# Attention with routed experts on one core: in the step that splits the next context, the keys projected in rounds 2 and 3, in the bank that the queries leave

## What is computed

```python
def xattn(query, key, value, ...):            # B = 8, S = 512, D = 512, H = 16, Hd = 32
    Q, K, V = split_heads(query @ Wq.T + bq), split_heads(key @ Wk.T + bk), split_heads(value @ Wv.T + bv)
    attn = softmax(einsum('bhqd,bhkd->bhqk', Q, K) / sqrt(Hd))
    return merge_heads(einsum('bhqk,bhkd->bhqd', attn, V)) @ Wo.T + bo
x = x + xattn(layernorm(x), ctx, ctx, ...)    # keys and values from the context
x = x + experts(layernorm(x), ...)            # router softmax, top 2 of 8, gated feed-forward, weighted sum
```

## Time and profile before

| | us |
|---|---|
| median of three executions | 1665.96 |
| lowest, highest | 1665.07, 1674.82 |
| the profiled execution | 1670.91 |
| its span in the trace | 1669.2 |
| PE busy | 1583.9 (95%) |
| DVE busy | 1308.7 (78%) |
| POOL busy | 836.0 (50%) |
| ACT busy | 692.8 (42%) |

### The profile page before, as it was taken

The page is one execution under the profiler, slowest core; times in us unless marked ns, Lnnn a source line. Parts: engine busy times, 40 slices in busy tenths (PEclk is TensorE's granted clock), DMA queues, the critical chain, the costliest instruction groups (busy, mean ns, idle before and its releaser), DMA issues. The chain is left out here.

```text
span 1669.2 us, 30419 instructions
## 1 busy us (share of the span) xinstructions
PE 1583.9 (95%) x9607; PEld 1162.8 (70%) x9607; DVE 1308.7 (78%) x2477; ACT 692.8 (42%) x1316; POOL 836.0 (50%) x628
## 2 busy tenths in 40 slices
PE   5898999999999999999998799979999999999996
PEld 4554555565555555655553398879999999999995
DVE  4576677877878778778796589988989879787885
ACT  3263544544545445445444253343334334233331
POOL 3355656566666666666678514232333333333322
PEclk9899999999999999999998899989999999999998
DMA  7342344353544443533343635644646346354433
GB/s 224 84 111 74 95 113 111 98 114 92 119 100 106 103 104 105 120 87 106 90 105 84 171 91 158 204 145 139 201 153 192 115 128 203 103 167 147 128 121 106
DMA packets 112246, 209.48 MB, mean 125 GB/s; under 512 B 32400, under 2 KB 33808, under 8 KB 112080
## 3 DMA queue, kind: packets, MB, share of 16 engines
q1 hardware_dynamic: 91248, 144.73, 31.8%
q0 software_dynamic: 20640, 62.49, 12.5%
q10 hardware_dynamic: 192, 0.26, 0.0%
HBM read 204.33 MB, written 37.51 MB: 145 GB/s over the span
## 5 line engine op out<-in xcount | busy, mean ns | idle before, releaser
L872 DVE TENSOR_REDUCE negmax<-max_ps 128x2 f32<-128x1024 f32 x252 | 306.9, 1218 | 150.0 <-PE max_ps L599 149.1
L730 ACT ACTIVATE pt<-work 128x512 f32<-128x512 f32 x512 | 277.5, 595 | 267.2 <-PE work L611 260.2
L1111 POOL TENSOR_TENSOR acc<-acc,pt 128x1024 f32<-128x1024 f32 x128 | 303.6, 2375 | 119.0 <-ACT pt L730 119.0
L1108 POOL TENSOR_TENSOR acc<-pt 128x1024 f32<-128x1024 f32 x64 | 153.4, 2398 | 187.6 <-PE work L631 118.2
L599 PE MATMUL max_ps<-ks,qs 96*128 96x512 f32 x504 | 195.7, 470 | 24.2 <-DVE negmax L872 13.3
L1494 PE MATMUL gu_ps<-xgT_hi,early_wg_hi 128*128 128x256 f32 x640 | 179.6, 281 | 1.5 <-DVE xgT_lo L1654 1.5
L1494 PE MATMUL gu_ps<-xgT_lo,early_wg_hi 128*128 128x256 f32 x640 | 177.6, 277 | 0.0
L1494 PE MATMUL gu_ps<-xgT_hi,early_wg_lo 128*128 128x256 f32 x640 | 177.5, 277 | 0.0
L611 PE MATMUL work<-qs,ks 98*128 98x512 f32 x512 | 170.4, 413 | 3.5 <-DMA qs<-m_lo 2.9
L1601 ACT ACTIVATE sig<-gate 128x256 f32<-128x256 f32 x156 | 65.0, 417 | 259.6 <-DVE gate L1664 258.8
L1494 PE MATMUL gu_ps<-xgT_hi,wg_hi 128*128 128x256 f32 x608 | 171.1, 281 | 1.3 <-DVE wg_lo L1452 1.3
(11 more groups left out here) (303 smaller groups left out, 3732.4 us busy)
## 6 DMA issues: line engine op xcount, KB each, us to landing
early_raw_g<-w_gate_up SPq DMA_DIRECT2D x39, 2048.0 KB
early_raw_d<-w_down SPq DMA_DIRECT2D x20, 1024.0 KB
raw_d<-w_down SPq DMA_DIRECT2D x19, 1024.0 KB
qs<-q_hi SPq DMA_DIRECT2D x252, 64.0 KB, 2.0
ks<-k_hi SPq DMA_DIRECT2D x252, 64.0 KB
bd<-b_down SPq DMA_DIRECT2D x39, 256.0 KB
x_in<-x SPq DMA_DIRECT2D x36, 256.0 KB, 3.2
ctxT_raw<-ctx_t SPq DMA_DIRECT2D x32, 256.0 KB, 4.1
```

What stands on the lines that cost most here:

```text
L730: e.activation(pt[k % 2][:, h, :], in_work("exp", u, k, h)[:, :], ACT.Exp, scale=scale).then_inc(exped.sem, 1)
L872: e.tensor_reduce(negmax[:, u % 2, n:n + 2], pair_of(u, r)[:, :, :], AX.X, ALU.max, negate=True).then_inc(maxed.sem, 1)
L1108: e.tensor_tensor(acc[:, heads, :], pt[0][:, heads, :], pt[1][:, heads, :], ALU.add).then_inc(added.sem, 1)
L1111: e.tensor_tensor(acc[:, heads, :], acc[:, heads, :], pt[k % 2][:, heads, :], ALU.add).then_inc(added.sem, 1)
```

## The change

In the splitting steps the low part of the queries is made one round earlier (2, not 3), and each half of the keys and values one round earlier too: keys in rounds 2 and 3, values in 4 and 5. The second half of the context's split moves the other way: `ctx_hi` of chunks 2 and 3 from round 1 to 2, `ctx_lo` of them from round 2 to 3. The keys' bank in these steps is the one that the queries leave, so its first use waits for `q_lo`. Below the inserted two lines every line of the changed kernel has a number one higher than in the kernel before (L872 is L873).

```diff
--- before.py
+++ after.py
@@ -329,13 +329,12 @@
                     at(6, ("v_out", u, 1))
                 elif c == 2:
                     at(0, ("q", u, 0), ("ctx_hi", b + 1, 0), ("ctx_hi", b + 1, 1))
-                    at(1, ("q", u, 1), ("ctx_hi", b + 1, 2), ("ctx_hi", b + 1, 3), ("ctx_lo", b + 1, 0), ("ctx_lo", b + 1, 1))
-                    at(2, ("ctx_lo", b + 1, 2), ("ctx_lo", b + 1, 3))
-                    at(3, ("low", u, "q"), ("k", u, 0))
-                    at(4, ("k", u, 1))
-                    at(5, ("low", u, "k"), ("v", u, 0))
-                    at(6, ("v_out", u, 0), ("v", u, 1))
-                    at(7, ("v_out", u, 1))
+                    at(1, ("q", u, 1), ("ctx_lo", b + 1, 0), ("ctx_lo", b + 1, 1))
+                    at(2, ("low", u, "q"), ("ctx_hi", b + 1, 2), ("ctx_hi", b + 1, 3), ("k", u, 0))
+                    at(3, ("ctx_lo", b + 1, 2), ("ctx_lo", b + 1, 3), ("k", u, 1))
+                    at(4, ("low", u, "k"), ("v", u, 0))
+                    at(5, ("v_out", u, 0), ("v", u, 1))
+                    at(6, ("v_out", u, 1))
                 else:
                     at(0, ("k", u, 0))
                     at(1, ("k", u, 1))
@@ -479,6 +478,8 @@
                 over, end = (Mark(whole_taken, (0,)), 0), ("whole_tiles",)
             if over:
                 bank = free.index(min(free))
+                if kind == "k" and what[0] > 1 and what[0] % C == 0:
+                    bank = free.index(at["low", what[0], "q"])
                 assert free[bank] < at[key], (key, ORDER[free[bank]])
                 uses.append((key, bank, *over))
                 free[bank] = at[end]
```

## The result

| | kernel before | changed kernel |
|---|---|---|
| median of six executions, us | 1666.24 | 1691.55 |
| lowest, highest | 1665.07, 1674.82 | 1684.16, 1694.04 |
| profiled execution, us | 1670.91 | 1694.04 |
| its span, us | 1669.2 | 1692.3 |
| start of step 31 in its trace, us | 902.5 | 924.8 |

The ratio is 1.0136, 95% interval 1.0117 to 1.0154: slower by over one per cent. On a second visit to a chip (experiment 8) the same kernel took 1685.05, ratio 1.0111 (1.0082 to 1.0140). The forecast of 1684.5 is nearer to the second; the first median stands 0.5 above the end of the range.

The account below looks back on a forecast made before the run. PE was taken to bound the kernel, losing 13 us in seven splitting steps. 16.3 + 2.0 - 2.3 + 5.2 - 2.35 = 18.85, taken as 18.5, moves the median from 1666.0 to 1684.5 us; range 1669 to 1691.

Parts of the forecast that it names:

- round 2: Splitting steps: the keys' first half waits 1.45 us for `q_lo`, so the round grows from 2.35 to 4.39, +2.04.
- round 3: Steps with `place`: the second `ctx_lo` stands behind POOL's first addition and delays the keys; 4.79 to 7.38 us, +2.59.
- rounds 6 and 7: End of a splitting step: round 6 loses its half of the values, -1.38 us, as in step 19.
- five steps with `place`, without the clock: Steps 10 to 26: 2.04 + 2.59 - 1.38 = 3.25 us each, 16.3 in all.
- steps 2 and 6: Splitting steps without `place`: 0.25 up to 1.6 us each, taken as 1.0 each, 2.0 together.
- stacking of `k_lo`, step 3: Start of step 3: its 2.27 us wait goes, as SP gets `k_lo` about a round earlier; -2.3 us once.
- clock in the five steps: After the five long waits: four falls of the granted clock to 1.2 GHz, 1.3 us each, 5.2 in all.
- one step in which POOL misses DVE: Round 3 of one of five steps: both `ctx_lo` pass before POOL asks, saving 2.35 us.
- the margin of 0.48: Round 3: 3.61 - 3.13 us; if `sum` is later by more than that, both `ctx_lo` pass before POOL's addition.
- Rival B: All the waits come but the clock doesn't fall: +16.0 us, or 13.6 with one miss, 1680 to 1682; chance 0.25.
- The 0.41 that round 3 was to give back: Steps 2 and 6, round 3: 0.41 us saved, since the `exp` matmuls no longer wait behind `ctx_hi` on ACT.
- What would show it: Signs named beforehand, among them a granted clock of 0.9 or less in several of the page's slices 8 to 20.

Follow-up runs that it names:

- experiment 8: The changed kernel itself, unaltered, timed once more on a second visit to a chip; 1685.05 us, ratio 1.0111 to the kernel before.
- experiment 3: The changed kernel without the choice of the bank, so the keys take the bank let go earliest; 1683.67 us, ratio 1.0127 to the kernel before.
- experiment 1: The changed kernel with the second pair of `ctx_lo` back in round 2, behind `q_lo`; 1666.94 us, ratio 1.0007 to the kernel before.
- experiment 2: The changed kernel with the second pair of `ctx_lo` still in round 3 but ahead of `place` on DVE; 1677.08 us, ratio 1.0069 to the kernel before.
- experiment 5: The changed kernel with nine spare full-width matmuls in round 3's long wait, steps 10 to 26; 1682.15 us, ratio 1.0105 to the kernel before.
- experiment 4: The changed kernel without the choice of the bank and with all of `ctx_lo` in round 2; 1663.97 us, ratio 0.9989 to the kernel before.
- experiment 7: The kernel of experiment 4 with two `x_in` loads moved to rounds 6 and 7, their statistics to the next step; 1655.92 us, ratio 0.9946 to the kernel before.
- experiment 9: The kernel before with only the two `x_in` loads moved to rounds 6 and 7, their statistics to the next step; 1664.55 us, ratio 0.9989.
- experiment 6: The kernel before with only the split's second halves a round later, keys and values where they were; 1673.81 us, ratio 1.0058.

## Why the prediction was right

The slowdown came by the mechanism and in about the size forecast. Each term against the traces of the changed kernel:

| term | predicted | measured |
|---|---|---|
| round 2 | +2.04 | +2.16 (4.51 against 2.35) |
| round 3 | +2.59 | +2.53 (7.32 against 4.79) |
| rounds 6 and 7 | -1.38 | -1.38 (6.71 against 8.09) |
| five steps with `place`, without the clock | 16.3 | 16.6 |
| steps 2 and 6 | 2.0 | 2.7 (2.01 and 0.70) |
| stacking of `k_lo`, step 3 | -2.3 | -3.3 |
| clock in the five steps | 4 x 1.3 | 5 x 1.55, and 4 falls in experiment 8 |
| one step in which POOL misses DVE | -2.35 | 0 |

**Round 2** went as written: `q_lo` ended 2.95 after the round's start, the keys' half began at 3.00 (3.01 was said), behind a wait of 1.45. Experiment 3 shows that it is the bank and not the data: without the choice the wait is 0.39. The 0.12 too little is the half itself, which took 1.51 and not 1.38.

**Round 3** rested on POOL's request falling between the two `ctx_lo`. `ctx_lo` started 3.00 after the round's start (said 3.01), POOL 3.14 (said 3.13). The second `ctx_lo` ended at 6.45 against 6.64. The rule of the Trainium skill ("SBUF — State Buffer", Who interferes with whom), that a VectorE instruction with two inputs in SBUF and a GpSimd instruction reading SBUF exclude each other whole instruction by whole instruction, holds here for L1108 (L1109 in the changed kernel) as well: 3.45 for the pair in the changed kernel, 1.29 in experiment 1, 2.58 for two tiny products in experiment 2.

**One miss** is the step that failed, a term of 2.35 that I put in by feeling. Ten long waits in two executions have no miss: the margin of 0.48 is wide for an order that repeats within 0.02.

**The clock** was mis-sized in price, 1.55 instead of 1.3. Rows 8 took the price from two rounds of step 3 whose work differs from step 19's; round 4 of step 14 in two executions of the changed kernel (3.89 with a fall, 2.35 without) is the better measure, and experiment 5, which fills the wait, confirms it. With five falls at 1.55 and no miss the same sum reads 16.3 + 2.0 - 2.3 + 7.75 = 23.75, and the profiled execution grew by 23.1. The two agree so well partly by chance, as the measured steps 2, 3, 6, 15 and 27 would make it 22.0, against 22.3 by the starts of step 31. Rival B (the clock holds) is what four steps of five did in experiment 3, and one of the changed kernel's ten.

**Steps 2 and 6** were taken at 1.0 each and took 2.0 and 0.7 more. The 0.41 that round 3 was to give back is 0.09 and 0.07 there, since those rounds were already short (4.48 and 4.46, against step 18's 4.79), and in step 2 rounds 6 and 7 gave back nothing (4.75 before and after).

**Stacking**: the wait of 2.27 in step 3 became 0.41, and a fall of the clock that followed it is gone, 3.3 in all. I had missed that steps 15 and 27 have the same wait (starts of 1.13 and 0.78), another 1.8. Step 0 (+1.6, where nothing is changed) and step 30 (-1.6, a fall of the clock at 885.9 that only the first trace has) are outside the change.

**What would show it** had one sign that couldn't: slices of the page below 0.9. A fall of 3.4 us takes 0.04 off a slice of 42, and every slice from 8 to 20 shows 9. The falls have to be read in stretches of their own length.

The total depends on how many falls an execution has. The first visit's executions were 6 us above the second's. Their mean granted clock averages 0.9797 against 0.9815, some 6 us more at 1.2 GHz in each, which by 1.55 for 3.4 us is an estimate of 3 of the 6; where the falls lie isn't known, since one execution each is traced, and the other 3 stay open. That the second median stands 0.5 from the forecast is luck: its trace has no miss and four falls of 1.55, 3.4 more than the sum, against which stand 2.8 less in steps 3, 15 and 27 and an experts' stage 2.7 shorter than that of the kernel before.

## What to carry to other kernels

Before a DVE operation with two SBUF inputs is moved, look what POOL does at its new place: a POOL addition of 2.4 us holds up an operation of 0.2 us as it does one of 0.6, and putting it in front of its neighbour only hands the collision to the neighbour (experiment 2). A step that looks free in one engine's order (keys a round earlier) has to be followed into the queue that carries its results: here it paid only together with a new order of SP's issues (experiments 4, 7 and 9), and of that gain the traces place some 2 us of 6 to 8 in the waits for SP.

## What the runs showed of the hardware

- The clock fell behind long waits in some executions and not in others. With the same waits around it, the long wait of round 3 (0.79, three matmuls, 1.80) was followed by a fall five times of five in the first profile of the changed kernel and four of five in the second; in experiment 3, where round 2's wait is 0.39 and not 1.45, once of five; in experiment 5, where nine matmuls fill the 1.80, never. Whether the shorter wait ahead or chance makes that difference wasn't tried. The Trainium skill ("TensorE: Matmul & The Clock Gate", Part 1) has it that the monitor runs free of the kernel; by that rule, equal waits may end either way, which fits steps 14 and 18 of experiment 8.
- `ln2` (L836 before, a tensor and two columns as scalars, 128 x 512) took 0.54 with POOL idle in the changed kernel, 1.62 beside POOL's second addition (567.55, 2.38 us) in experiment 2 and 1.48 beside it (566.88, 2.48 us) in experiment 6, and both times it ended 0.3 after POOL did. It has one tensor input of full width, so two such inputs aren't the only case; whether it is the scalars' columns or something else wasn't tried.
